# A graph network of four layers: every layer's node work put beside the gathers in 1024-row batches, edge results kept in the order of the edge slots

## What is computed

```python
x = _layernorm(x + appnp(x))     # 10 rounds of out = spmm(out) * 0.9 + h * 0.1, over edges by src
x = _layernorm(x + gcn(x))       # segment_sum of (x @ W) * norm, with self loops, + b, then prelu
x = _layernorm(x + cheb(x))      # see below
x = _layernorm(x + gine(x))      # two convs: h = x + segment_sum(relu(x[src] + e)); relu(relu(h@W1+b1)@W2+b2)
```

## Time and profile before

| | us |
|---|---|
| median of 3 runs | 19613.53 |
| lowest, highest | 19551.92, 19645.81 |
| profiled execution, its span | 19500.54, 19498.6 |
| PE busy | 4989.7 (26%) |
| DVE busy | 7925.3 (41%) |
| ACT busy | 4445.0 (23%) |
| POOL busy | 9261.5 (47%) |

### The profile page before, as it was taken

One profiled execution on the slowest core, in us unless ns is written; L12 is line 12 of the kernel. 1 busy time (PEld: TensorE's weight loads), 2 busy tenths in 40 slices (PEclk: granted clock), 3 DMA queues, 4 the chain that ended last, 5 costly groups with the idle time before them and its releaser, 6 DMA issues. The chain is left out here.

```text
span 19498.6 us, 112697 instructions
## 1 busy us (share of the span) xinstructions
PE 4989.7 (26%) x21148; PEld 3673.9 (19%) x21148; DVE 7925.3 (41%) x22330; ACT 4445.0 (23%) x12525; POOL 9261.5 (47%) x9572
## 2 busy tenths in 40 slices
PE   0013100000000000000006500466655406665566
PEld 0002100000000000000005400244444304443344
DVE  7540224333343333227118722100356682362465
ACT  0000222111111111016124422333211151241231
POOL 0734456565656556761760166555100005456657
PEclk9955555555555555555555555677777756656555
DMA  5403423322333333116115422222233364453453
GB/s 169 156 32 151 147 71 102 98 89 89 95 99 92 93 91 90 49 60 233 32 29 181 158 66 65 69 66 66 97 118 118 122 212 136 156 180 121 141 168 105
DMA packets 882044, 2149.88 MB, mean 110 GB/s; under 512 B 323642, under 2 KB 335621, under 8 KB 860033
## 3 DMA queue, kind: packets, MB, share of 16 engines
q1 hardware_dynamic: 539648, 1558.93, 23.5%
q0 software_dynamic: 325760, 507.15, 9.5%
q10 hardware_dynamic: 16128, 78.68, 1.0%
HBM read 1267.25 MB, written 916.16 MB: 112 GB/s over the span
## 5 line engine op out<-in xcount | busy, mean ns | idle before, releaser
L547 POOL DMA_INDIRECT hop_odd_raw<-hop_table,i_hop x1176 | 1112.4, 946 | 589.2 <-issue 394.8
L547 POOL DMA_INDIRECT hop_even_raw<-hop_table,i_hop x1176 | 1112.3, 946 | 580.1 <-issue 362.0
L547 POOL DMA_INDIRECT cheb_raw<-cheb_table,i_cheb x784 | 748.4, 955 | 309.0 <-issue 236.3
L600 DVE SCALAR_TENSOR_TENSOR cheb_total<-cheb_ends,dst_joins,cheb_rows 128x96 f32<-128x96 f32 x168 | 54.7, 326 | 1937.2 <-ACT cheb_rows L646 1362.8
L1322 PE MATMUL cheb_mixing<-folded,cheb_hops_turned 96*128 96x292 f32 x2352 | 825.4, 503 | 0.0
L1969 POOL DMA_DIRECT2D mid<-cheb_nodes_rows x56 | 30.0, 535 | 1637.2 <-DVEq L2368 1637.2
L1011 POOL DMA_INDIRECT own_raw<-x,i_dst x392 | 370.9, 946 | 902.8 <-POOLq L88 563.2
L2190 PE MATMUL cheb_nodes_product<-folded,cheb_nodes_turned_rows 97*128 97x292 f32 x1568 | 550.7, 502 | 695.5 <-DVE cheb_nodes_mixed L2336 592.8
L600 DVE SCALAR_TENSOR_TENSOR hop_odd_total<-hop_odd_total,src_joins,hop_odd_rows 128x96 f32<-128x96 f32 x1008 | 328.5, 326 | 944.7 <-remote 582.1
L600 DVE SCALAR_TENSOR_TENSOR hop_even_total<-hop_even_total,src_joins,hop_even_rows 128x96 f32<-128x96 f32 x1008 | 328.4, 326 | 938.6 <-remote 529.7
L1214 POOL DMA_INDIRECT mixed<-cheb_mixed,dst_end x392 | 384.2, 980 | 638.3 <-ACT cheb_mixed L1348 535.9
(11 more groups left out here) (481 smaller groups left out, 21538.2 us busy)
## 6 DMA issues: line engine op xcount, KB each, us to landing
mixed<-map_dst_fill SPq DMA_DIRECT2D x56, 2044.0 KB
cheb_nodes_mixed<-mixed SPq DMA_DIRECT2D x56, 2044.0 KB
hop_odd_res<-hop_table SPq DMA_DIRECT2D x168, 336.0 KB
hop_table<-hop_odd_sums SPq DMA_DIRECT2D x168, 336.0 KB
hop_even_res<-hop_table SPq DMA_DIRECT2D x168, 336.0 KB
hop_table<-hop_even_sums SPq DMA_DIRECT2D x168, 336.0 KB
start_x<-x_and_map SPq DMA_DIRECT2D x56, 700.0 KB
x<-start_normed ACTq DMA_DIRECT2D x56, 700.0 KB
```

The costliest lines, as they stand in the source:

```text
L547: pool.indirect_dma_start(out=raw_rows[:, b % RAW, g, :], out_offset=None, in_=table, in_offset=bass.IndirectOffsetOnAxis(ap=index[:, t:t ...
L600: nc.vector.scalar_tensor_tensor(into, before, side.joins[:, t:t + 1], rows[:, w, g, :], ALU.mult, ALU.add).then_inc(s["chained"], 1)
```

## The change

- `NodePass`, `run_node_pass` and its four passes, `MixHops`, the norm helpers, the fill of `mixed` and of the table `sums` go. Every node stage is now a job of a class below `Rows`: `StartRows`, `GcnRows`, `ChebRows`, `NormRows` beside `GineRows`, in batches of 1024 rows, with the norm of `GineRows`.
- The sums of gcn and of all three Chebyshev passes are stored in slot order. Rows of nodes without an edge are right from the dense job alone; rows of nodes with one are worked out again for the slots (`..._slots`) and scattered over them. So `own` moves ahead of gcn and gathers x1, `x2_slots`, `mid_slots` and `x3_slots` are kept, and a separate gather of x3 is gone.
- Dense jobs stand beside gathers: GCN low beside own, high beside gcn; Chebyshev's x term, softmax and sums low beside cheb1, high beside cheb2; the whole first convolution of the fourth layer and the norm of the slot rows beside gine1.
- The three terms' product of the slots is put aside beside cheb3 (`part_out`), the fourth term is added in cheb_slots (`part_in`). Batch norm takes its sums from products of the rows with themselves (97 columns a group, `gram`). The edge weight of the Chebyshev passes is split in a factor for the source (`w_cheb`) and one for the sum (`f_cheb`, applied by ScalarE when it copies the totals).
- In a pass with jobs, `meets` and its root are issued two batches ahead (`lag`). cheb_norm's first multiply is done by GpSimd (`by_pool`), and its last and start's by ScalarE. In `own_rows` VectorE keeps one value of each gathered row, and GpSimd waits for that (`kept`).

```diff
-        run_node_pass(nc, k, StartPass(nc, k, "start", xj, hop_sums, x1))
-        edge_pass(nc, k, "gcn", by_dst, Scatter(nc, k, sums), x1, by_dst.other, weight=k.w_gcn, scale=k.s_gcn,
-                  fix_scale=k.fix_gcn[:, 0:1], meets=(ALU.add, 1.0))
+        batches, slots = NP // (P * Rows.GROUP), (0, EP // (P * Rows.GROUP))
+        low, high = (0, batches // 2), (batches // 2, batches)
+        slot_rows(nc, k, "start", StartRows(nc, k, "x1", (0, batches), xj, hop_sums, x1))
+        own_rows(nc, k, "own", x1, k.i_dst, x1_slots, k.own_degree,
+                 (GcnRows(nc, k, "base", True, low, x1, *layer, x2, turned_by_act=True),))
+        edge_pass(nc, k, "gcn", by_dst, Store(nc, k, hop_a), x1, by_dst.other, weight=k.w_gcn, scale=k.s_gcn,
+                  fix_scale=k.fix_gcn[:, 0:1], meets=(ALU.add, 1.0),
+                  jobs=(GcnRows(nc, k, "base", True, high, x1, *layer, x2, turned_by_act=True),))
...
-        run_node_pass(nc, k, GcnPass(nc, k, "gcn_nodes", x1, sums, W, b, slope, x2))
+        slot_rows(nc, k, "gcn_slots", GcnRows(nc, k, "ends", False, slots, x1_slots, *layer, x2_slots, sums=hop_a,
+                                              scatter=(by_dst, x2, k.N - 1), turned_by_act=True))
...
+        propagate("cheb1", cheb_a, x2, by_dst.other,
+                  (ChebRows(nc, k, "base", True, low, [(0, x2)], mid, gram=(total, True)),))
+        propagate("cheb2", cheb_b, cheb_a, k.i_cheb,
+                  (ChebRows(nc, k, "base", True, high, [(0, x2)], mid, gram=(total, False)),))
+        propagate("cheb3", cheb_c, cheb_b, k.i_cheb,
+                  (ChebRows(nc, k, "part", False, slots, [(0, x2_slots), (1, cheb_a), (2, cheb_b)], mixed, part_out=True,
+                            turns=2, copies=("act", "dve", "dve")),))
+        slot_rows(nc, k, "cheb_slots", ChebRows(nc, k, "ends", False, slots, [(3, cheb_c)], mid_slots, part_in=mixed,
+                                                gram=(total, False), turns=2, scatter=(by_dst, mid, k.N - 1)))
+        batch_norm(nc, k, gamma, beta)
+        slot_rows(nc, k, "cheb_norm", NormRows(nc, k, "x3", True, (0, batches), x2, mid, x3, by_pool=True))
...
         edge_pass(nc, k, "gine1", by_dst, Store(nc, k, sums1), x3, by_dst.other, added=feats,
-                  jobs=(GineRows(nc, k, "low", True, (0, half), conv, second, out, skip=x3, turned_by_act=True),))
+                  jobs=(GineRows(nc, k, "conv", True, (0, batches), x3, first, conv, also=(conv_low, low[1])),
+                        NormRows(nc, k, "x3", False, slots, x2_slots, mid_slots, x3_slots)))
+        slot_rows(nc, k, "gine1_slots", GineRows(nc, k, "ends", False, slots, x3_slots, first, conv_slots, sums=sums1,
+                                                 scatter=(by_dst, conv, k.N - 1), banks=1),
+                  (GineRows(nc, k, "base", True, low, conv_low, second, out, skip=x3, banks=1, turned_by_act=True),))
```

More of the change, by code:

```diff
@@ L605, in _ @@
                         job.vector(ph, dve, q)
+            for job in jobs:
+                job.vector_end(ph, dve)
         @block.tensor
@@ L623, in _, with take_root @@
         def _(act):
+            def take_root(b):
+                act.wait_ge(s["met"], 2 * b + 2)
+                nc.scalar.activation(root[:, b % WORK, :], degree[:, b % WORK, :], ACT.Sqrt).then_inc(s["rooted"], 1)
             for job in jobs:
                 job.scalar_setup(ph, act)
+            if meets is not None:
+                for b in range(lag):
+                    take_root(b)
             for b in range(batches):
@@ L740, in store @@
             return
-        m = i % self.DEPTH
-        rows, stored = self.rows[:, m, :, :], self.sem(ph, f"stored{m}")
-        sp.wait_ge(self.sem(ph, "ready"), i + 1)
+        rows, stored = self.what(i), self.sem(ph, f"stored{i % self.DEPTH}")
+        self.made(ph, sp, i)
         start = (self.first + i) * self.GROUP * P
@@ L755, in store @@
             sp.dma_start(self.view(self.out, i), rows).then_inc(stored, 16)
+            if self.also is not None and self.first + i < self.also[1]:
+                sp.dma_start(self.view(self.also[0], i), rows).then_inc(stored, 16)
     def pieces(self, i):
@@ L759, in pieces @@
         if not self.dense or start + self.GROUP * P <= self.out.shape[0]:
-            return 1
+            return 1 + (self.also is not None and self.first + i < self.also[1])
         left = max(self.out.shape[0] - start, 0)
@@ L802, in pool @@
         m = i % self.DEPTH
[L803 removed]
+        self.made(ph, pool, i)
         pool.nop(nofuse=True)
@@ L2429, in batch_norm @@
         wide = ph.psum("wide_rows", [P, 512])
+        mean, square, root, shift = (moment[:, n:n + 1] for n in range(4))
         block = ph.block()
@@ L2596, in graph_layers @@
-        slot_rows(nc, k, "gine2_slots", GineRows(nc, k, "last", False, slots, conv_slots, second, None, sums=sums2,
+                  jobs=(GineRows(nc, k, "base", True, high, conv, second, out, skip=x3, turned_by_act=True),))
+        slot_rows(nc, k, "gine2_slots", GineRows(nc, k, "ends", False, slots, conv_slots, second, None, sums=sums2,
                                                  skip=x3_slots, scatter=(by_dst, out, k.N - 1)))
```

1559 lines of the change are left out of this document (671 added, 888 removed).

## The result

The changed kernel takes 18,200.5 us (median of 4 runs, 18,170.9 to 18,211.7), the kernel before 19,613.1: a ratio of 0.928 with a 95% interval of 0.926 to 0.931. The forecast was 18,743 (a ratio of 0.956), with 17,950 to 19,500 as the range and 0.79 for faster. Direction and range hold; the gain is 7.2% where 4.4% was forecast.

What follows compares the result with a forecast made beforehand. It took no engine to fill any rewritten stage, handoffs arriving late while Pool issues indirect DMAs. Stage terms summed to −785, with setup −865: 18,635 profiled, scaled to 18,743 us; range 17,950 to 19,500.

Steps and rivals of the forecast that it cites:

- five signs: Features near 200 us, gcn rounds 11 to 12, cheb1 TensorE over 500, cheb3 near 1150, VectorE idle under a quarter in gine1.
- cheb3: Third Chebyshev pass: 1150 us in place of 1520, from TensorE's half-steps plus 200 and some 50; bounds 950 and 1470.
- about 900 at 0.7: TensorE's 98 half-steps in cheb3: 1264 us at 1.2 GHz, 632 at 2.4, about 900 at a clock of 0.7.
- Rival B: TensorE holds 2.4 GHz in cheb1, cheb2, cheb3, gine1, gine1_slots: −750 us, cheb3 −230 of it, total 18,000; chance 0.2.
- The rule rounds × work + 200: Stages with 392 Pool DMAs: rounds times a round's work plus 200 us for late handoffs, never below Pool's 490.
- cheb1's round: cheb1 and cheb2: TensorE sets a round of 10.4 us, VectorE and ScalarE lie beside it; 780 us each, bounds 650 and 1000.
- cheb_norm: Chebyshev norm stage: 600 us in place of 552, with 80 for Pool's multiply delaying VectorE; bounds 520 and 700.
- start: First node stage: 98 batches at 4.5 us of VectorE, 445 us in place of 418; said it can't be below 400.
- Setup: Features behind the map scatter without the 56 fill DMAs: −80 us, bounds −150 and 0.
- Rival C: Handoffs stop while Pool gathers: 5.2 us a round more in own, gcn, cheb1 to 3, gine1; +1730, 20,500; chance 0.22.
- The scaling by 113 us: Whole kernel: the median of the runs lies 113 us (0.6%) above the profiled execution, taking 18,635 to 18,743.

Runs made afterwards that it cites:

- the experiment: Changed kernel with the dense Chebyshev rows in a stage of their own ahead of cheb1, cheb1 and cheb2 without a job: the three took 1918 us in place of 1436.
- the run without lead: Changed kernel with gcn's degree, root, reciprocal and weighing in line in each round, nothing issued ahead: gcn with the preparation took 814 us in place of 792.
- the run of half the lead: Changed kernel with GpSimd gathering at most 4 batches ahead instead of 8: 15,722 us, ratio 0.943, where the kernel before took 16,676.
- half the lead gave 292 us: The kernel of all edits (without jobs in turn in gine1_slots) with GpSimd at most 4 batches ahead instead of 8: 17,465 us, ratio 0.891.
- all edits: Changed kernel plus cheb_norm's multiply on VectorE, start's join ahead, jobs in turn, three product buffers, later exponent: 15,251 us (0.914) on one chip, 17,757 (0.905) elsewhere.

## Why the prediction was right, and where it was off

The mechanism was right: work that stood alone now stands beside gathers whose engines idled (482 us by the experiment), and the large Chebyshev stages shrink. The sum was 439 us too high on the profiled execution, and of the five signs that the prediction gave for being right one held: features after the scatter near 200 us (194). gcn's round was 12.8 to 13.4 us, not 11 to 12; TensorE was busy 426 us in cheb1, not over 500; cheb3 took 926, not near 1150; VectorE idled 41% of gine1, not under a quarter. That the total came out inside the range is thus partly terms that missed on either side. By its own terms:

- *cheb3* was the largest miss, 224 us. The step that failed is "about 900 at 0.7". PE busy 691 at a granted 0.89 gives 98 × 7.05; the 200 us of loss on top were in place (926 - 691 = 235). The stage even fell below the lower bound of 950. Rival B's number for this stage, −230, was right, and in this stage alone: gine1 and gine2 got 0.60 and 0.51. gine2 took 42 us more with no change to its code (726 against 684, both up to the first instruction of gine2_slots; the 675 of before ends 10 us earlier); how much of that is the clock isn't shown, and the same code took 701 to 730 us in the runs on such chips.
- *The rule rounds × work + 200* took one loss for every stage. It is no constant: by the two chips it is 53 us in gcn and 64 in gine1, 115 in cheb1 and cheb2, and 154 to 186 in own, cheb3 and gine2. One part lies at the start of a pass, where one round takes 45 us (gcn) to 81 us (cheb3) while GpSimd issues unbroken. In gcn, whose rounds stay above GpSimd's 8.75 us, little more is lost, as the run without lead showed. Where a round is shorter than that, slow ones follow: in cheb3 a round of 24 to 27 us behind each one of 7.7, where the other chip has 14.3, and in cheb1 16 and 28 behind 6.2. Where the rule came out right (gine1, 1251 for 1250) two errors cancelled: less loss, and rounds of about 21 us instead of 18.8, because the jobs' order kept TensorE and VectorE from overlapping. gcn was 83 too high with rounds of 13 instead of 11.5 and about 50 us of loss instead of 200. gine1_slots was 79 too high, half of it loss and half work: the run of half the lead had it at 570 us on the other chip, against the 610 of the sum, and 161 were lost.
- *cheb1's round* was put down to TensorE (10.4). It is VectorE and ScalarE in series or VectorE alone, 12.6 and 9.5; TensorE at 0.74 was busy 426 of 718 us, 7.6 a round. That is what the prediction's own figures give, 11.2 us at 0.5 being 7.8 at the 0.72 of own; its 10.4 goes with a clock of 0.54, which it gave no reason for. The 10.4 was still near the mean round, by another cause: the run of half the lead took 610 us for each of the two stages on the chip without late handoffs, 10.9 a round. With about 108 us of loss instead of 200 the stages came out 62 below the forecast.
- *cheb_norm*: 681 against 600. I had taken 80 of contention between bounds of 0 and 180; it was 98 × 1.0 on the addition, and on top came 78 us of idling on the squares, which I hadn't counted. The Trainium skill's rule ("SBUF — State Buffer", "Who interferes with whom") described the held addition, and the trace agrees: 949 ns without GpSimd's multiply, 1952 beside it. The 690 that its pages gave came nearer by luck: it had a hold of 1.7 us a batch, which was 1.0, since VectorE's addition begins when part of GpSimd's multiply is over, and it had no idling on the squares.
- *start*: 470 against 445, the same idling on the squares, 0.80 us a batch. The statement that it can't be below 400 was wrong: VectorE's work is 3.84 us a batch, not 4.1, and with the join ahead the stage took 384.
- *Setup*: features 115 us faster instead of 80. Another 76 came in the sort, which I had at nothing, and rightly, as the fills put back show.
- *Rival C*, handoffs that stop while GpSimd gathers, is real but smaller than I priced it, 5.2 us a round in six passes on top of my 200 each. By the two chips those six passes lose 53 to 174 us each, less than even the 200. It is there in passes without a job too (21.0 against 4.3 us a round in the hops, 105 us in hop_ninth).
- The scaling by 113 us from the profiled execution to the median added 108 us of error: the changed kernel's profiled execution (18,197.5) lies at its median (18,200.5).

## What to carry to other kernels

Before laying two engines' work side by side in a sum, follow one round through each engine's queue: an instruction that waits holds all behind it, and here such an order cost 206 us with two jobs in blocks, 18 to 70 with an exponent behind mixing, and 86 in start alone with a reduction ahead of free work, at nearly unchanged busy times. Work given to an idle GpSimd isn't free beside two-input VectorE instructions. A lead of gathers deeper than needed can cost time where the other engines hardly move while GpSimd issues: half the lead gave 292 us. And a stage's loss isn't all the kernel's: the unchanged kernel before was 15% shorter on one chip.

## What the runs showed of the hardware

- On all chips here but one, waits of ScalarE and VectorE, even VectorE's for its own previous instruction, ended late while GpSimd issued indirect DMAs without a pause: 21.0 us a round against 4.28 without, in the same pass of the same execution.
- Not on every chip: on one, the same hop pass took 503 us instead of 599 to 607, and the kernel before 16,676 us instead of 19,512 to 19,613. The ratio of a change depends on it: all edits gave 0.914 there and 0.905 elsewhere (the latter without jobs in turn in gine1_slots).
- VectorE's two-input addition of 768 elements took 1952 ns beside GpSimd's multiply of 1869 ns, and 949 alone.
- GpSimd's gathers took longer beside VectorE's instructions with two inputs of 768 elements (TENSOR_TENSOR): in cheb1 and cheb2 of the changed kernel 0.94 us alone or beside the chain, and 1.68 beside the second addition, a mean of 59. GpSimd was busy 447 us in cheb1 for that, instead of 377 before the change:

```profile
11504.22 0.96 DVE L1315 TENSOR_TENSOR cheb_base_rows<-cheb_base_rows,cheb_base_weighted 128x768 f32<-128x768 f32 x1
11504.44 1.55 POOL L542 DMA_INDIRECT cheb_raw<-x,dst_other  x1 [0.30 <-issue]
11505.21 0.96 DVE L1317 TENSOR_TENSOR cheb_base_rows<-cheb_base_rows,cheb_base_weighted 128x768 f32<-128x768 f32 x1
11506.30 0.94 POOL L542 DMA_INDIRECT cheb_raw<-x,dst_other  x1 [0.30 <-issue]
```

- The sort by destination varied from 589 to 707 us between executions of unchanged code at about 497 us of VectorE work in each.
